# Value stores on eight semaphores, four of their quads one stage later, and half as many gather rests

## The reference

```python
kw = kT[src, :, etype]                          # gather a key per edge
m = vT[src, :, etype]                           # gather a value per edge
a = jnp.einsum('ehd,ehd->eh', kw, q[dst]) * pri[:, etype].T / SQRT_D
att = edge_softmax(a, dst, n)                   # over the edges of one dst
msg = (m * att[:, :, None]).reshape(-1, H * HS)
hag = jax.ops.segment_sum(msg, dst, num_segments=n)
```

## Time and profile before

| | us |
|---|---|
| median of 3 runs | 6388.16 |
| lowest, highest | 6379.66, 6402.51 |
| the profiled execution | 6379.74 |
| its span | 6377.7 |
| score stage, layer 0: first gather, last issue of one | 4209.4, 4773.0 |
| score stage, layer 1: first gather, last issue of one | 5453.8, 6019.7 |

### The profile page before, as it was taken

The page is one execution under the profiler, slowest core; times in us unless marked ns, Lnnn a source line. Parts: engine busy times, 40 slices in busy tenths (PEclk is TensorE's granted clock), DMA queues, the critical chain, the costliest instruction groups (busy, mean ns, idle before and its releaser), DMA issues. The chain is left out here.

```text
span 6377.7 us, 51889 instructions
## 1 busy us (share of the span) xinstructions
PE 3273.2 (51%) x13857; PEld 2271.0 (36%) x13857; DVE 2150.2 (34%) x5081; ACT 1006.9 (16%) x2209; POOL 3215.0 (50%) x3406
## 2 busy tenths in 40 slices
PE   5555677667774555633363434643424446344263
PEld 3333555445553333333242322222324322233253
DVE  3222322232224222411121113532437545233385
ACT  0000322232222111200010002410004424000063
POOL 4665466646663676366646663036660330566503
PEclk7666776776777777755575556765657768555586
DMA  2111333334332332211131115985753569666453
GB/s 62 47 46 41 84 99 99 101 81 100 100 100 81 90 92 84 106 47 47 46 130 47 45 47 204 423 274 165 201 167 106 161 259 425 214 188 194 137 149 95
DMA packets 630966, 826.34 MB, mean 130 GB/s; under 512 B 93076, under 2 KB 510342, under 8 KB 618134
## 3 DMA queue, kind: packets, MB, share of 16 engines
q1 hardware_dynamic: 480117, 492.37, 23.0%
q0 software_dynamic: 120608, 276.12, 16.2%
q10 hardware_dynamic: 29952, 54.54, 2.8%
HBM read 470.63 MB, written 352.04 MB: 129 GB/s over the span
## 5 line engine op out<-in xcount | busy, mean ns | idle before, releaser
L480 POOL DMA_INDIRECT arena<-table,idx_s x3128 | 2995.3, 958 | 2351.0 <-issue 1104.0
L752 PE MATMUL ps<-arena,work 128*128 x4160 | 967.7, 373 | 1043.9 <-issue 937.7
L752 PEld LDWEIGHTS ps<-arena,work 128*128 128x128 f32 x4160 | 814.3, 271 | 1303.7 <-issue 1166.8
L1974 PE MATMUL ps<-arena,work 128*128 x1664 | 414.7, 385 | 681.7 <-issue 585.0
L1974 PEld LDWEIGHTS ps<-arena,work 128*128 128x128 f32 x1664 | 343.0, 280 | 754.5 <-issue 654.6
L460 DVE TENSOR_SCALAR work<-iota_row,dl_s,w_s 128x128 f32<-128x128 f32 x1248 | 350.7, 360 | 455.0 <-issue 325.0
L456 DVE TENSOR_TENSOR work<-ps,dl_s 128x512 f32<-128x512 f32 x208 | 143.8, 691 | 928.5 <-issue 601.7
L1943 DVE TENSOR_TENSOR arena<-arena,ps 128x128 f32<-128x128 f32 x832 | 182.4, 280 | 732.4 <-issue 332.6
L930 DVE SCALAR_TENSOR_TENSOR arena<-ps,vecs,arena 128x256 f32<-128x256 f32 x208 | 100.5, 483 | 891.5 <-issue 415.3
L1834 PE MATMUL ps<-arena,onehot 32*128 32x512 f32 x1600 | 292.4, 855 | 117.8 <-DVE arena L1871 57.6
L511 PE MATMUL ps<-work,picks 128*104 128x512 f32 x416 | 313.2, 840 | 54.7 <-issue 52.0
(11 more groups left out here) (331 smaller groups left out, 3529.2 us busy)
## 6 DMA issues: line engine op xcount, KB each, us to landing
table<-arena SPq DMA_DIRECT2D x96, 2048.0 KB
onehot<-col_rows ACTq DMA_DIRECT2D x208, 256.0 KB
values<-arena SPq DMA_DIRECT2D x832, 64.0 KB
arena<-values SPq DMA_DIRECT2D x208, 256.0 KB
arena<-table,idx_s POOLq DMA_INDIRECT x3128
arena<-edge_times SPq DMA_DIRECT2D x208, 128.0 KB
edge_part<-arena SPq DMA_DIRECT2D x208, 128.0 KB
table<-arena SPq DMA_DIRECT2D x50, 512.0 KB
```

Of the source, the lines that this page charges most:

```text
L480: pool.indirect_dma_start(ring[:, ds(t % RING * 2 * H, width)], None, tab, bass.IndirectOffsetOnAxis(ap=idx_s[:, t:t + 1], axis=0)).then_i ...
L752: mm = pe.matmul(accf[:, ds(b, P)], o, arena[:, ds(slot, H)], start=False, stop=False, skip_group_check=True)
L1974: mm = pe.matmul(ps[:, n % 8, c * P:(c + 1) * P], across_ring[:, n % DEEP, c * P:(c + 1) * P], Qn_flat[:, ds(b, P)], start=True, stop=True)
```

## The change

Four edits, all in the score and softmax stages of both layers:
- The value stores take turns on eight semaphores in place of four, so that a quad waits for the quad eight before it. GpSimd's `freed` waits on the same ones.
- The stores of the last four quads (100 to 103) are issued by SyncE in the softmax stage. The score stage's queue ends when quads 92 to 95 are stored. DVE waits for quads 96 to 103 ahead of its first backward scan.
- So that nothing unstored is overwritten, `ahead` moves to the tensor `work` and `wide` to the end of `arena`.
- GpSimd rests at every eighth tile quad in place of every fourth.

```diff
+OUTS = 8
+LATE = 4
...
-            ahead = arena[:, 10928:10928 + LINKS]
+            ahead = work[:, 3 * NP - 4 * DEEP * P:3 * NP - 4 * DEEP * P + LINKS]
...
+            def store_values(sp, n, rows_in):
+
+                if n >= OUTS:
+                    sp.wait_ge(ring_out[n % OUTS].sem, ring_out[n % OUTS].at(64 * (n // OUTS)))
+                slot_regs, slots = step_slots(sp, n * 4, 4, behind=(H,))
+                for s in slots:
+                    sp.lower_ap(arena[:, ds(s, H)])
+                if rows_in is not None:
+                    sp.wait_ge(rows_in.sem, step_need(sp, n) + rows_in.base)
+                for c in range(4):
+                    sp.dma_start(values[ds(n * 4 + c, 1), :, :].rearrange("a e f -> (a e) f"),
+                                 arena[:, ds(slots[c], H)]).then_inc(ring_out[n % OUTS].sem, 16)
+                release(sp, slot_regs)
...
-                                pool.wait_ge(ring_out[m % QUADS].sem, ring_out[m % QUADS].at(64 * (m // QUADS + 1)))
+                                pool.wait_ge(ring_out[m % OUTS].sem, ring_out[m % OUTS].at(64 * (m // OUTS + 1)))
                             stored_quads[0] = n
-                        gathers(pool, table32, 2 * H, freed, rest=4)
+                        gathers(pool, table32, 2 * H, freed, rest=8)
...
-                        trips(sp, body)
-                        for q in range(QUADS):
-                            sp.wait_ge(ring_out[q].sem, ring_out[q].at(64 * TRIPS))
+                        for n in range(ALL_QUADS - LATE):
+                            store_values(sp, n, arrived)
+                        for n in range(ALL_QUADS - LATE - OUTS, ALL_QUADS - OUTS):
+                            sp.wait_ge(ring_out[n % OUTS].sem, ring_out[n % OUTS].at(64 * (n // OUTS + 1)))
...
-                wide = arena[:, 14256:14256 + STEPS * HEADS].rearrange("p (g x) -> p g x", g=GSTEPS)
+                wide = arena[:, 20600:20600 + STEPS * HEADS].rearrange("p (g x) -> p g x", g=GSTEPS)
                 with nc.Block() as block:
+                    @block.sync
+                    def _(sp):
+                        for n in range(ALL_QUADS - LATE, ALL_QUADS):
+                            store_values(sp, n, None)
+                        for n in range(ALL_QUADS - OUTS, ALL_QUADS):
+                            sp.wait_ge(ring_out[n % OUTS].sem, ring_out[n % OUTS].at(64 * (n // OUTS + 1)))
+
...
                         ch(scan_f(link, -BIG, ALU.max, turned_scores))
+                        for n in range(ALL_QUADS - OUTS, ALL_QUADS):
+                            dve.wait_ge(ring_out[n % OUTS].sem, ring_out[n % OUTS].at(64 * (n // OUTS + 1)))
                         scan_b(link, -BIG, ALU.max, ahead).then_inc(copied.sem, 1)
```

More of the change, by code:

```diff
@@ L1895, in freed @@
                             for m in range(stored_quads[0] + 1, n + 1):
-                                pool.wait_ge(ring_out[m % QUADS].sem, ring_out[m % QUADS].at(64 * (m // QUADS + 1)))
+                                pool.wait_ge(ring_out[m % OUTS].sem, ring_out[m % OUTS].at(64 * (m // OUTS + 1)))
                             stored_quads[0] = n
-                        gathers(pool, table32, 2 * H, freed, rest=4)
+                        gathers(pool, table32, 2 * H, freed, rest=8)
                     @block.sync
                     def _(sp):
-                        def body(i, first):
-                            for q in range(QUADS):
[L1904 to L1914, removed]
-                        trips(sp, body)
-                        for q in range(QUADS):
-                            sp.wait_ge(ring_out[q].sem, ring_out[q].at(64 * TRIPS))
+                        for n in range(ALL_QUADS - LATE):
+                            store_values(sp, n, arrived)
+                        for n in range(ALL_QUADS - LATE - OUTS, ALL_QUADS - OUTS):
+                            sp.wait_ge(ring_out[n % OUTS].sem, ring_out[n % OUTS].at(64 * (n // OUTS + 1)))
                     @block.scalar
@@ L1986, in score_phase @@
                     s.base += ALL_QUADS
-                for s in ring_out[0:QUADS]:
-                    s.base += 64 * TRIPS
             def softmax_phase():
-                wide = arena[:, 14256:14256 + STEPS * HEADS].rearrange("p (g x) -> p g x", g=GSTEPS)
+                wide = arena[:, 20600:20600 + STEPS * HEADS].rearrange("p (g x) -> p g x", g=GSTEPS)
                 with nc.Block() as block:
+                    @block.sync
[4 more added lines that the diff above has]
+                            sp.wait_ge(ring_out[n % OUTS].sem, ring_out[n % OUTS].at(64 * (n // OUTS + 1)))
                     @block.vector
@@ L2087, in _ @@
                         turn_steps(pe, scan_in.rearrange("p (g e) -> p g e", e=P), {0: 5, 3: 6}, evac)
+                for s in ring_out[0:OUTS]:
+                    s.base += 64 * (ALL_QUADS // OUTS)
                 mixed.base += 2
```

## The result

The changed kernel took 6424.83 us (median of six runs, 6400.06 to 6430.07) against 6373.23 us for the kernel before (six runs, 6360.6 to 6402.51): ratio 1.0068, 95% interval 1.0051 to 1.0085. It was forecast at 6365, with 0.18 on slower. The fourth rival is what happened. Run again in two later jobs, the same two kernels gave 1.0062 once, and once 0.987, near the third rival's figure. What sets the two outcomes apart in the traces is whether the instruction queues are slowed while gathers run. I call that the mode. The first trace showed it, and I had priced it wrongly.

What follows compares the result with a forecast made beforehand. GpSimd's gathers were busiest, with SyncE's slowed store queue last in layer 0's score stage. Late stores -23.7, DVE's waits +0.4, semaphores 0 and rests 0 gave -23.3 us: 6388.16 to 6365 us, range 6312 to 6405.

Steps and rivals of the forecast that it cites:

- fourth rival: Score stage: the store queue starves at 6.1 us a quad, +16 us a layer, 6420 us; chance 0.18.
- third rival: Score stage: GpSimd alone sets the pace, 80 us less over both layers, 6308 us; chance 0.22.
- case 4: The store queue starves, chance 0.18; its sign is quad 99 finished later than 591 us from the first gather.
- Eight semaphores: Value stores in the score stage: removes a wait put at nothing, taken as 0, gain at most 1.7 us.
- Late stores: Score stage's end: moving four quads' stores to softmax gains 12.7 and 11.0 us, hidden before the backward scan.
- Rests: Score stage: 12 of 24 rests go, 28 us of GpSimd's time a layer, but stalls move to gates; taken as 0.
- the ring: Score stage: quad k's gather waits for quad k-9's store, so the store queue falls only nine quads behind.
- gates: GpSimd's waits for stores and DVE, replacing rests; 2 to 5 us each, growing from some 15 to 40 us a layer.
- the pace settles near the present one: Score stage: gates let the store queue catch up like rests, so it stays near 5.81 us a quad.
- The cause of the slowness: Score stage: stores slow with distance from a rest while gathers run, 2.9 us a quad around one, 9.0 far behind.
- the deciding pace: Store queue in the score stage: 5.94 us a quad, where layer 0 gains nothing; the present pace was 5.81.
- Who is slowed: Score stage: SyncE's store queue is slowed while gathers run, and TensorE shows the same, 4 matmuls in 11 us.

Runs made afterwards that it cites:

- after: The profiled execution of the changed kernel in the first comparison; it took 6400.06 us.
- outs4: The changed kernel with four semaphores for the stores in place of eight; ratio 1.0071 to the kernel before, 6429.76 us.
- rest4: The changed kernel with the rest put back to every fourth quad; ratio 0.9979 to the kernel before, 6373.24 us.
- before_third: The kernel before, unedited, run once more in the fifth follow-up job for its trace; 6382.0 us, one run.
- before: The profiled execution of the kernel before in the first comparison; it took 6379.74 us.
- before_again: The kernel before, unedited, run once more in the fourth follow-up job; 6309.04 us, one run.
- after_again: The changed kernel, unedited, run once more in the fourth follow-up job; ratio 0.987 to the kernel before, 6228.24 us.
- split8: The changed kernel with the stores of the odd quads issued from ScalarE's queue; ratio 0.9967 to the kernel before, 6397.81 us.
- narrow8: The changed kernel gathering 128 floats a row in place of 256; 6421.51 us in one run, beside 6419.44 for the kernel before.

## Why the prediction was wrong, point by point

Its own mark for case 4 was quad 99 later than 591 us behind the first gather: it is 606.2 in after.

- *Eight semaphores, 0*: right (outs4). No store waits for a store in any trace.
- *Late stores, -23.7 us*: right in mechanism. The backward scan started 13.4 to 14.8 us into softmax in the traces of both kernels, never held. As a size it held beside the new rests (24 us), seems to be some 10 beside the old (rest4's ratio with all else is worth 13), and is nothing without the steps. It hangs on how far the queue is behind at the stage's end, and I took that from one execution: quad 95 was issued 565 us behind the first gather in its layer 0, but at 541 in its layer 1, and at 542 and 541 in before_third.
- *Rests, 0*: **this step failed**. Measured alone it is +70 us (1.0109), or +59 as outs4 over rest4 (1.0071 against 0.9979 in one job). The mechanism stood in the prediction: the queue falls behind, the ring is full, gates take the rests' place. The fault is the sentence "the pace settles near the present one": it went from 5.81 to 6.11 us a quad in layer 0, and quad 99 was stored 28.2 us later, just what the fourth rival says. Two costs were left out. A gate is dearer than a rest: it opens when a late queue has issued and landed a store or DVE has multiplied, 4.7 us on average in layer 0 of after and up to 7.7, where a rest costs 2.3. The gates cost 56 and 68 us in the two layers of after, where I had them grow to some 40. And with gates in charge the queue stays far behind, so the stage ends with a backlog of some 20 us, which I had named as what speaks *against* the fourth rival.
- *The cause of the slowness*: the rows around one rest were read rightly, but as a law of the hardware. It is a mode. Without it GpSimd alone sets the pace, and the third rival's sum is met to within 3 us, with its parts off as said above. One trace could not show that the mode may be absent. It could show how near the edge the kernel was: the margin to the deciding pace was 5.94 - 5.81 = 2%, and I gave 0.18 to crossing it when 12 of the 24 pauses that held the queue up were to go.
- *Who is slowed*: I had only SyncE and TensorE. DVE's queue steps as well, four times as often in after as in before.
- *Range*: 6312 to 6405 lies between the modes. It misses the 6424.8 measured, and would have missed the other mode's gain too (6388 less 82 is 6306). The far part of either of two rivals was cut off to come down to 8 in 10.

What sets the mode stays open. Kernel, inputs and code are the same, and it was the same in all traces of one job. Each job had a chip of its own and none was tried twice, so it may go with the chip, the time, or whatever else is set once a job. Three of the gathering passes outside the two stages also took 552 to 559 us in before and 540 to 546 in before_again. No trace shows what occupies the queues. Loading of instructions doesn't look like it: while layer 0's gathers ran there were 31 packets on the instruction queues in after and 32 in after_again.

## What to carry over

A pause that looks like waste may be what lets another queue catch up; before you thin it out, work out what takes its place when the slow queue is full, and price that wait by its own length, and the backlog that is left at the end. Where a queue issues late and waits for nothing, count its instructions and look at the duration of a register operation. And run a change whose worth hangs on such a queue in more than one job, on different chips: here the same two kernels gave 1.0068, 0.987 and 1.0062.

## What I had not expected of the hardware

- While 128-row gathers are issued back to back, the instructions of SyncE's, TensorE's and DVE's queues, register operations too, can take steps of 0.70 us, and ScalarE's where it issues stores (split8). GpSimd's gathers keep their pace, and DVE's arithmetic its duration. In after, SyncE started 2.6 instructions per us in the first 5 us behind a pause of over 2 us, 1.2 between 13 and 18 us, and 0.7 between 18 and 28. Without the mode it kept 2.1 between 13 and 18.
- The mode was there in the comparison and three jobs, and absent in two. Medians of the kernel before were 6373 to 6419 us with it, 6294 and 6311 without.
- Halving the bytes of each gather changed neither its time (944 ns, median) nor the slowing (narrow8).
